# Twice the memory for GpSimd's transfer descriptors, and two of its three drains taken out of the expert part

## The reference

```python
x = x + xattn(layernorm(x), ctx_1024, ctx_1024)        # causal softmax attention within a sequence, scale 128**-0.5
h = layernorm(x)
logits = h @ gate_w.T                                  # 8 experts
_, idx = top_k(logits + beta, 2)
c = zeros.at[token, idx].add(sigmoid(logits[idx]))     # weight of each of the two chosen experts
eo = (silu(h @ gate_proj[e]) * (h @ up_proj[e])) @ down_proj[e]      # per expert, M = 256
x = x + sum_e c[e] * eo[e] + (silu(h @ sg) * (h @ su)) @ sd          # experts and one shared expert
```

## Time and profile before

| | |
|---|---|
| Time, median of 3 runs | 432.77 us |
| Lowest and highest of the 3 | 430.17 and 433.64 us |
| Span of the profiled execution (the page gives no other time of it) | 435.0 us |
| PE busy | 393.7 us (91%) |
| DVE busy | 292.4 us (67%) |
| POOL busy | 255.6 us (59%) |
| ACT busy | 240.3 us (55%) |
| Mean DMA rate | 96 GB/s |

### The profile page before, as it was taken

The page is one execution under the profiler, slowest core; times in us unless marked ns, Lnnn a source line. Parts: engine busy times, 40 slices in busy tenths (PEclk is TensorE's granted clock), DMA queues, the critical chain, the costliest instruction groups (busy, mean ns, idle before and its releaser), DMA issues.

```text
span 435.0 us, 11130 instructions
## 1 busy us (share of the span) xinstructions
PE 393.7 (91%) x3325; PEld 327.7 (75%) x3325; DVE 292.4 (67%) x1273; ACT 240.3 (55%) x570; POOL 255.6 (59%) x317
## 2 busy tenths in 40 slices
PE   8888999999799798796877789999999999999994
PEld 3444666657455564686867689999999999999993
DVE  5877998897697486564654366666667766666663
ACT  3696989879687462334343356666311256666550
POOL 7758788785688577046878855555420005555554
PEclk9999999999999899898989989999999999999999
DMA  7973337793221112225557763333333212332222
GB/s 218 357 226 120 123 130 232 229 265 125 67 92 52 64 50 82 87 69 120 97 86 88 72 95 45 48 52 51 49 58 71 52 27 36 49 49 32 26 26 24
DMA packets 43049, 41.78 MB, mean 96 GB/s; under 512 B 5688, under 2 KB 31808, under 8 KB 42992
## 3 DMA queue, kind: packets, MB, share of 16 engines
q1 hardware_dynamic: 30864, 30.69, 24.4%
q0 software_dynamic: 12128, 10.40, 17.5%
HBM read 24.17 MB, written 16.90 MB: 94 GB/s over the span
## 4 chain that ended last, share of the span: by engine, by line
PE 53%; POOL 5%; DVE 5%; issue 4%; another core or an unknown queue 2%; POOLq 1%; ACT 0%; DVEq 0%; ACTq 0%
PE gu_pair L1710 32%; PE bank L1734 16%; POOL sorted_rows L495 3%; PE bank L1676 2%; DVE t_hid L1275 1%; PE bank L1649 1%; POOL rstd L455 1%; PE bank L1637 1%; POOL out L546 1%; PE bank L1628 0%; DVE hid L1106 0%; ACT rows L734 0%; POOLq L493 0%; DVE x L1025 0%
## 5 line engine op out<-in xcount | busy, mean ns | idle before, releaser
L546 POOL DMA_INDIRECT out<-t_out,tile_in x64 | 100.4, 1569 | 108.0 <-DVE t_out L1315 100.2
L1710 PE MATMUL gu_pair<-tile_T,W_slot 128*128 128x128 f32 x1024 | 129.5, 280 | 1.5 <-issue 0.9
L1710 PEld LDWEIGHTS gu_pair<-tile_T,W_slot 128*128 128x128 f32 x1024 | 123.6, 197 | 1.9 <-issue 1.7
L831 ACT ACTIVATE t_silu<-gu_pair 128x512 f32<-128x512 f32 (+1 forms) x78 | 46.4, 594 | 125.7 <-PE gu_pair L1710 109.5
L1734 PE MATMUL bank<-W_down,t_hid 128*128 (+1 forms) x620 | 84.6, 280 | 14.1 <-DVE t_hid L1275 14.1
L1275 DVE SCALAR_TENSOR_TENSOR t_hid<-t_silu,gu_pair 128x512 f32<-128x512 f32 (+1 forms) x78 | 53.2, 683 | 62.6 <-PE gu_pair L1710 29.9
L1734 PEld LDWEIGHTS bank<-W_down,t_hid 128*128 128x128 f32 x620 | 76.7, 195 | 16.2 <-issue 16.2
L495 POOL DMA_INDIRECT sorted_rows<-rows,slot x64 | 64.6, 1009 | 21.8 <-issue 20.7
L821 ACT ACTIVATE W_slot<-W 128x512 f32 x128 | 73.0, 621 | 3.4 <-DVE slot_pair L1166 2.0
L506 POOL DMA_INDIRECT left_in<-sorted_rows,left_index x27 | 26.1, 967 | 23.0 <-DVE left_index L1193 15.0
L1649 PE MATMUL bank<-shared_dn,hid 128*128 128x128 f32 x256 | 34.6, 293 | 1.0 <-DVE hid L1106 0.9
(11 more groups left out here) (160 smaller groups left out, 551.2 us busy)
## 6 DMA issues: line engine op xcount, KB each, us to landing
tile_in<-sorted_rows SPq DMA_DIRECT2D x91, 66.5 KB, 1.9
x_sb<-x SPq DMA_DIRECT2D x16, 256.0 KB, 5.0
c_T<-ctx_cols SPq DMA_DIRECT2D x16, 256.0 KB
c_sb<-ctx SPq DMA_DIRECT2D x16, 256.0 KB
out<-acc SPq DMA_DIRECT2D x16, 256.0 KB
sorted_rows<-padding SPq DMA_DIRECT2D x1, 2128.0 KB, 13.0
sorted_rows<-left_in SPq DMA_DIRECT2D x27, 66.5 KB
sorted_rows<-rows,slot POOLq DMA_INDIRECT x64
```

Of the source, the lines that this page charges most:

```text
L546: e.indirect_dma_start(out_flat, bass.IndirectOffsetOnAxis(ap=tile_in[:, tiles_of(i)[0] % NR, ID:ID + 1].bitcast(I32), axis=0), t_out[:, q ...
L831: e.activation(t_silu[:, 0:n * M], gate_up_pair[i % 2][0][:, 0:n * M], ACT.Silu).then_inc(s_t_silu, 1)
L1710: r = e.matmul(bank[:, c:c + P], w, tile_T[:, i % TX, tile], start=True, stop=True, skip_group_check=True)
```

## The change

The two drains inside GpSimd's loop over the slots go. The drain between the scatters and the loop stays. No other instruction of any engine is added, removed or moved.

```diff
--- before.py
+++ after.py
@@ -720,8 +720,6 @@
                     gather_left(j)
                 gathered = left_before(q)
                 add_to_out(q)
-                if q in (FULL - 1, SLOTS - 11):
-                    e.drain()
             for q in range(SLOTS - NR, SLOTS):
                 e.wait_ge(s_t_added[q % NR], 16 * (q // NR + 1))
 
@@ -1992,7 +1990,7 @@
     import concourse.bacc as bacc
     from concourse.bass_utils import run_bass_kernel_spmd
 
-    nc = bacc.Bacc("TRN2", target_bir_lowering=False, num_devices=1)
+    nc = bacc.Bacc("TRN2", target_bir_lowering=False, num_devices=1, dynamic_dma_scratch_size=32768)
     arrays, args = {}, []
 
     def by_rows(a, n, m):
```

## The result

The changed kernel takes 438.76 us (median of 4 runs, 437.87 to 443.47), the kernel before 432.50 us beside it (430.17 to 433.64): a ratio of 1.0167, 95% interval 1.0108 to 1.0225, so 6.3 us more. The forecast was 432.8 us with 429.0 to 436.5; the time lies above that range.

What follows compares the result with a forecast made beforehand. From 255 to 428 us PE was taken to set the pace, with GpSimd having time to spare. Both drains and the doubled memory counted 0 + 0 + 0, leaving the median, 432.8 us, range 429.0 to 436.5 us.

Steps and rivals of the forecast that it cites:

- The first and the second drain: Drains behind slots 36 and 53: removal gains 0; one lies beside 40.11 us of waiting, the other's 2.32 us is made up.
- The sum: Whole kernel: 0 each for both drains and the doubled memory, leaving the median, 432.8 us.
- rival 2: Program's end: settles 81 more transfers at 0.09 us each, 7.4 us, giving 440.2 us, 1.7% slower; chance 0.05.
- a fixed time to notice that transfers are done explains 1.55 us as well: Second drain, behind slot 53: its 1.55 us beyond landing could be fixed, not 0.09 us for each of 17 transfers.
- the 440.2 us: Program's end: the time if the final drain settles 81 more transfers, 432.8 + 7.4 us.
- the wait for landing (1.3 us): GpSimd's adds: an add lands about 1.3 us behind its end, subtracted from the second drain's 2.85 us.
- PE's product at 426.52 us: End of the expert part: taken as PE's last down product, 0.91 us long, setting GpSimd's last add at 430.38 us.
- Rival 1: Adds from slot 37 on: GpSimd waits for room, up to 2.85 us in the last three, 435.7 us; chance 0.07.
- Rival 3: Gather stage: larger memory removes 0.30 us gaps, 0.9 us a slot over ten slots, 423.8 us, 2.1% faster; chance 0.05.
- The doubled memory: Descriptor memory: no wait for room seen, gaps 0.30 us throughout; doubling it and moving tensors by 16384 bytes taken as 0.

Runs made afterwards that it cites:

- the drain behind slot 59: The kernel before (16384 bytes, two drains in the loop) with a third drain added behind slot 59: 432.50 us, ratio 0.9981.
- the drain behind slot 57: The kernel before (16384 bytes) with its second loop drain moved four slots later, from slot 53 to slot 57: 434.68 us, ratio 0.9997.

## Why the prediction was wrong

**The first and the second drain: right as read.** The places where they stood behaved as the working said: 40.11 us behind slot 36 unchanged, the add of slot 54 0.28 us behind its data (398.78 us is DVE's result of slot 53, 401.17 that of slot 54, and 401.17 + 0.35 + 0.28 = 401.80), and no consumer earlier for it. As waits they were worth 0.

**The sum: the step that failed.** "0 + 0 + 0" costed the drains as waits alone. They did work too, 64 transfers' settling at the first (5.28 us) and 17 at the second, and the program's end contains a drain that does what they leave. The missing term is 81 transfers at 0.0817 us with nothing beside them, 6.6 us. The prediction had it as rival 2, worked out from the drain behind slot 53 to 0.09 us each and 7.4 us in all, so mechanism and size were on the page, 12% too high; what failed was its chance, 0.05. I gave it so little for one sentence, "a fixed time to notice that transfers are done explains 1.55 us as well". The fixed part of the final drains is 0.05 us. The views left both readings of that number open, and even then something like even chances would have been fair, with the 440.2 us inside the range. But the trace of before could choose. It has the records of its own drains: 7.071 us behind slot 36 with 64 transfers, 4.222 us behind slot 53 with 17, each behind a single add of 1.55 us. A fixed time would have made them equal; the longer one also shows that what the first drain takes can be seen.

That the price came so near is partly luck. The working took the wait for landing (1.3 us) and the settling as one after the other, and the restart as the usual 0.30 us. In the record the drain behind slot 53 ends 2.44 us behind its add, where 1.3 and 1.44 would be 2.74, and the restart takes 0.72 us. The two errors nearly cancel.

**A reading that was off, without a part in the miss:** PE's product at 426.52 us isn't its last. The last ends at 428.61 us, DVE's last `t_out` is there at 429.44, and the last add starts 0.94 us behind that, since it follows the add before it by the usual 0.30 us. So the end of the adds hangs in part on GpSimd's own pace, as the drain behind slot 59 showed.

**Rival 1** (the wait comes back inside the adds) exists, but hardly: stops of 0.19 us with 16384 bytes, one of 0.74 us without any drain at 32768, and none in the changed kernel. So it has no part in the 6.3 us.

**Rival 3** fell. With the memory doubled the gaps stayed at 0.30 us, and a slot beside the gathers at 4.48 us on GpSimd. And at the lower level of the times PE is full there while GpSimd's slots take as long (last section), so GpSimd's pace alone isn't what holds PE there.

**The doubled memory: 0** was right within 0.1% on its own. In the change it did harm by being there: with the drains out, 16384 bytes cost 5.4 us and 32768 bytes 6.6 us at the tail, since more memory keeps more transfers for the end. The Trainium skill's statement cited in the prediction ("DMA: Bandwidth & Descriptors", section "SWDGE vs HWDGE vs iDMA": a ring that the DMA engines empty) speaks of room alone. No run here shows GpSimd held up for room for more than 0.74 us at one place. What the change should have weighed isn't room but what is left to settle.

What stays open: what exactly is settled, and why a short stop deals with 42 transfers in 0.74 us or 15 in 0.19 us, 0.013 to 0.018 us each if they were settled there, where a drain takes 0.0817. Also open is what sets the number at which such a stop comes; the 73rd transfer since a drain with 16384 bytes, seven places from the 114th to the 137th transfer of the program with 16384 bytes and no drain, and the 129th with 32768 don't fit one rule that I could show.

## What to carry to other kernels

A drain of GpSimd is not only a wait: here it took longer by 0.0817 us for each indirect transfer since the last one, and at the end of the program that time has no cover. Before taking out a drain that looks idle, ask who does its work then, and look at the time from the last transfer's landing to the end of the span; put a drain where the engine waits anyway, with few transfers behind it but enough slots to make up the delay. Where a trace gives one duration for a price that may be fixed or by the piece, look for a second instance with another number of pieces (here the drain's own records); if there is none, the range has to hold both.

## What the runs showed of the hardware that wasn't expected

- GpSimd's drain at the end took 0.05 us and 0.0817 us for each indirect transfer since the drain before it, though all had landed (in the changed kernel it begins at 429.3 us, when the DMA engines are idle). In the loop, drains for 64 and 81 transfers ended 5.28 and 6.67 us behind the add before them, on the same line.
- Less memory for descriptors made the end shorter. With both drains out the final drain took 7.483, 6.217 and 1.726 us at 32768, 16384 and 4096 bytes, and even 4096 bytes made no gap more than 0.3 us longer than its likes among 27 gathers and 64 adds.
- The kernel before took 399.15 us in one set of runs and 432.99 and 434.24 us in two others. Windows of 190 to 255 us, of the kernel with the loop's two drains out and 16384 bytes (lower level), and of that with the drain behind slot 57 (higher level):

```profile
190.00:255.00 65.00, 64.97 (x580) 64.56 (x580) 44.35 (x134) 39.14 (x71) 52.51 (x41) 1.00 0.65 88
```

```profile
190.00:255.00 65.00, 50.45 (x362) 47.20 (x362) 31.17 (x115) 23.95 (x44) 47.40 (x41) 0.89 0.60 89
```

In the first PE is full beside the gathers, at the full clock and a DMA share of 0.65; in the other it gets through 362 matrix products for 580, with a granted clock of 0.89 and a DMA share of 0.60. A slot takes GpSimd 4.47 to 4.50 us in both. So the waiting of PE that I had laid beside GpSimd's pace comes with the level of the times, and its cause wasn't found. The tail with ten transfers left is 3.0 us at the lower level (the kernel with the memory doubled) and 3.1 us at the higher one.
